# Joining two adjacency pieces on GpSimd before TensorE packs them, in a four-layer graph attention kernel

## The reference

```python
Wh = h @ W
e = (Wh @ a1)[:, None] + (Wh @ a2)[None, :]
e = jnp.where(e >= 0, e, ALPHA * e)
scores = jnp.where(adj > 0, e, NEG_BIG)
attention = jax.nn.softmax(scores, axis=1)
return attention @ Wh
```

## Time and profile before

| | |
|---|---|
| median of 3 executions | 4015.39 us (4013.88 to 4015.58) |
| the profiled execution, its own time | 4017.89 us |
| its span, first to last instruction | 4016.0 us |
| mean granted TensorE clock | 0.991 |
| layer 0 within the span | about 72 to 1107 us |
| instructions | 88535 |

### The profile page before, as it was taken

How to read it: one execution, slowest core, us unless ns; L and a number is a source line. 1 busy time by engine, 2 the same in 40 slices (tenths; PEclk the granted TensorE clock), 3 DMA queues, 4 the chain that set the end, 5 groups by cost and what they waited for, 6 DMA issues and landing times.

```text
span 4016.0 us, 88535 instructions
## 1 busy us (share of the span) xinstructions
PE 3924.8 (98%) x37901; PEld 3914.9 (97%) x37901; DVE 3621.3 (90%) x7914; ACT 1128.7 (28%) x2397; POOL 10.2 (0%) x98
## 2 busy tenths in 40 slices
PE   6999999999999999999999999999995999999999
PEld 6999999999999999999999999999995999999999
DVE  6888888888889999999998999999997999999998
ACT  6666666666641111111133111111112000000000
POOL 0000000000000000000000000000000000000000
PEclk9999999999999999999999999999997999999999
DMA  7787878787700000000001000000000000000000
GB/s 221 263 273 261 273 260 274 260 269 265 240 12 14 17 12 17 14 17 12 14 12 56 17 14 16 12 14 17 12 12 11 12 14 17 14 14 14 17 14 12
DMA packets 163146, 332.41 MB, mean 83 GB/s; under 512 B 12608, under 2 KB 87488, under 8 KB 162752
## 3 DMA queue, kind: packets, MB, share of 16 engines
q1 hardware_dynamic: 162752, 326.75, 24.8%
HBM read 305.53 MB, written 21.17 MB: 81 GB/s over the span
## 4 chain that ended last, share of the span: by engine, by line
PE 95%; DVE 2%; ACT 2%; issue 1%; POOL 0%; DVEq 0%; POOLq 0%; ACTq 0%
PE acc L1047 90%; PE ps_pack L983 2%; PE ps_wh L1065 1%; ACT vals L1219 1%; PE ps_wh L1059 1%; DVE q L676 0%; DVE q L842 0%; DVE q L850 0%; DVE vals L558 0%; DVE mask L649 0%; ACT adj_bf L1146 0%; DVE q L538 0%; PE acc L1109 0%; PE ps_bc L1022 0%; PE acc L1001 0%
## 5 line engine op out<-in xcount | busy, mean ns | idle before, releaser
L1047 PE MATMUL acc<-vals,q 128*128 128x129 f32 x32640 | 3731.2, 276 | 8.3 <-DVE q L676 8.3
L1047 PEld LDWEIGHTS acc<-vals,q 128*128 128x128 f32 x32640 | 3679.7, 192 | 9.9 <-issue 9.2
L676 DVE SCALAR_TENSOR_TENSOR q<-rrow,R,mask 128x512 f32<-128x512 f32 x3968 | 2840.6, 749 | 227.0 <-PE acc L1047 78.5
L1146 ACT ACTIVATE adj_bf<-adj_int,threshold 128x1024 bf16<-128x1024 int32 x512 | 584.2, 1143 | 119.5 <-PE ps_pack L983 79.0
L649 DVE TENSOR_SCALAR mask<-bits 128x512 uint16<-128x512 uint16 (+1 forms) x2080 | 444.5, 292 | 8.7 <-DMA rrow<-rows 4.6
L1230 ACT ACTIVATE xnew<-acc,rec 128x128 f32<-128x128 f32 x248 | 70.4, 365 | 899.3 <-DVE rec L707 802.9
L983 PEld LDWEIGHTS ps_pack<-packer,adj_bf 128*128 128x128 bf16 x4096 | 140.7, 96 | 8.1 <-ACT bits L1153 3.5
L983 PE MATMUL ps_pack<-packer,adj_bf 128*128 128x32 bf16 x4096 | 142.6, 176 | 4.3 <-ACT bits L1153 3.3
L1237 ACT ACTIVATE e<-xnew 128x512 f32<-128x512 f32 x48 | 30.3, 631 | 397.6 <-DVE xnew L737 314.2
L1250 ACT ACTIVATE e<-xnew,nm,rs 128x128 f32<-128x128 f32 x193 | 79.4, 481 | 216.9 <-DVE nm L530 216.9
L1245 ACT ACTIVATE sd<-ve 128x4 f32<-128x4 f32 (+1 forms) x49 | 9.9, 202 | 363.3 <-DVE ve L511 363.3
(11 more groups left out here) (186 smaller groups left out, 853.6 us busy)
## 6 DMA issues: line engine op xcount, KB each, us to landing
adj_int<-in_adj_dram SPq DMA_DIRECT2D x512, 512.0 KB, 4.7
rrow<-rows SPq DMA_DIRECT2D x60, 256.0 KB, 3.2
x_between_layers<-xnew SPq DMA_DIRECT2D x32, 256.0 KB, 4.0
xin<-x_between_layers SPq DMA_DIRECT2D x32, 256.0 KB, 2.7
xin<-in_x_dram SPq DMA_DIRECT2D x16, 256.0 KB, 4.8
wh_of_layer<-wh SPq DMA_DIRECT2D x1, 4096.0 KB, 16.9
x_of_layer<-xnew SPq DMA_DIRECT2D x16, 256.0 KB, 2.3
xin<-x_of_layer SPq DMA_DIRECT2D x16, 256.0 KB, 2.7
```

The lines of the kernel that those rows point to most:

```text
L676: nc.vector.scalar_tensor_tensor(q[:, j % RING, :], row, column(R_, t), mask[:, c % 2, j, :], ALU.max, ALU.mult).then_inc(q_ready, 1)
L1047: last = nc.tensor.matmul(to, q[:, j % RING, b * P:(b + 1) * P], vals[:, t, :], start=first, stop=(t == KT - 1 or g.two and t == EARLY - 1 ...
L1146: nc.scalar.activation(adj_bf[:, n % BIN_RING, :], adj_int[:, n % ADJ_RING, :], ACT.Sign, bias=threshold[:, 0:1], accum_out=degree_parts[: ...
```

## The change

GpSimd gets a function `joined(n)`. It waits until pieces n and n + 1 (two blocks of rows, same columns) are converted, multiplies the second by 4 in place, waits for that, and adds it to the first in place. As the powers of two of block b + 1 are four times those of block b, the packing matmul of the joined piece with the packer of block b yields the sum of both packings. TensorE waits for `adj_joined` in place of `adj_binary`, packs the first slot of each pair alone, and raises `adj_packed` by 2. GpSimd does the first 8 joins ahead of the first maximum over partitions, the joins of pieces 16 to 501 ahead of the second, and the last five pairs ahead of the third.

```diff
+            def joined(n):
+                pool.wait_ge(adj_binary, n + 2)
+                first, second = adj_bf[:, n % BIN_RING, :], adj_bf[:, (n + 1) % BIN_RING, :]
+                nc.gpsimd.tensor_scalar(second, second, 4.0, None, ALU.mult).then_inc(adj_times_4, 1)
+                pool.wait_ge(adj_times_4, n // 2 + 1)
+                nc.gpsimd.tensor_tensor(first, first, second, ALU.add).then_inc(adj_joined, 1)
+
             starts = [WHOLE[0], SOON[1], LATE[1], SOON[2], LATE[2]]
+            for n in range(0, LEAD * QP, 2):
+                joined(n)
             for n, to in enumerate([scales(st)[0][:, :] for st in starts] + [found[:, 0:1], found[:, 1:2], S[:, :]]):
+                if n == SOON[1].n:
+                    for i in range(LEAD * QP, GROUPS * PIECES - LEAD * QP + 6, 2):
+                        joined(i)
+                if n == LATE[1].n:
+                    for i in range(GROUPS * PIECES - LEAD * QP + 6, GROUPS * PIECES, 2):
+                        joined(i)
                 pool.wait_ge(smax_ready, n + 1)
                 nc.gpsimd.partition_all_reduce(to, smax[:, :], P, RMAX).then_inc(S_ready, 1)
...
             def pack(v, c, n):
                 if n == 0:
                     need(pe, bits_ready, v * CHUNKS + c)
-                for i in range(n, n + BATCH):
-                    pe.wait_ge(adj_binary, v * PIECES + (c * QP + i + 1))
+                for i in range(n, n + BATCH, 2):
+                    pe.wait_ge(adj_joined, (v * PIECES + c * QP + i) // 2 + 1)
                     for t in range(PT):
                         at = (i // BLOCKS * PT + t) * WORDS
                         last = nc.tensor.matmul(ps_pack[:, at:at + WORDS], adj_bf[:, i % BIN_RING, t * P:(t + 1) * P],
                                                 packer[:, i % BLOCKS, :], start=(i == 0 and t == 0),
-                                                stop=(i == QP - 1), skip_group_check=True)
-                    last.then_inc(adj_packed, 1)
+                                                stop=(i == QP - 2), skip_group_check=True)
+                    last.then_inc(adj_packed, 2)
```

More of the change, by code:

```diff
@@ L285, in build @@
         adj_binary = sem("adj_binary")
+        adj_times_4 = sem("adj_times_4")
+        adj_joined = sem("adj_joined")
         adj_packed = sem("adj_packed")
```

## The result

The changed kernel takes 4663.32 us (median of 3 executions, 4662.97 to 4663.39) against 4015.39 before: 1.1614 times as long, 95% interval 1.1592 to 1.1637. The forecast was 4615, range 4100 to 4880. In this document a run given with one time is a single execution; nine executions of the kernel before lie between 4013.50 and 4018.22 us.

What follows compares the result with a forecast made beforehand. TensorE bounds the kernel before; after the change VectorE and GpSimd were to share one resource. 4017.89 + 583 (sweeps) + 15 (start-up) + 2 (stall at layer 0's end), less 2.5 for the median, gives 4615 us, range 4100 to 4880.

Steps and rivals of the forecast that it cites:

- The bound and the slack: Layer 0 sweeps: TensorE bounds at 4.06 us a period, 0.40 of it packing; VectorE works 3.39, 0.67 to spare.
- Who pays for a join: Layer 0: VectorE's product with two SBUF inputs and a GpSimd read lock each other out; VectorE has 0.47 us spare.
- case (a): Kernel before: the all-reduce to S_early, issued behind a product of L676, was held about 0.53 us until that product ended.
- case (b): Kernel before: an unpacking issued behind 64 GpSimd memsets takes 1.44 us instead of 291 ns, ending 0.15 after them.
- The price of a join: GpSimd's multiply and add per pair: streams of 0.89 and 1.78 us plus 0.70 fixed, 3.4 us when alone.
- The sum: Layer 0 sweeps: VectorE's 3.39 plus 2.67 plus half of 0.70 makes 6.41 us a period against 4.06, +583 us.
- Start-up: Eight pairs ahead of layer 0: 6.6 us apart instead of 5.12, 10 us, plus some 3 before the all-reduce; +15 taken.
- A finer sharing: Layer 0: engines alternate element by element, 5.4 us a period, +332, some 4365 us; with a partial hold, chance 0.20.
- Nobody held: Layer 0: GpSimd reads leave products alone, TensorE stays the bound, 3978 us; held below break-even included, chance 0.13.
- The clock: Layer 0: TensorE's clock at 0.50 makes its work 7.7 us a period, +905, about 4940; with dear GpSimd, chance 0.07.
- GpSimd dearer than its memsets: Layer 0 joins: GpSimd far slower than its memset rows, streams of 4.45 us, 5055 us; with the clock, chance 0.07.

Runs made afterwards that it cites:

- the multiply aside: Kernel before, with GpSimd multiplying 1024 bf16 elements on scratch once per pair for 208 pairs, nothing waiting for it: 4025.82 us.
- the add aside: Kernel before, with GpSimd doing a two-input add on scratch once per pair for 208 pairs, nothing waiting for it: 4225.22 us.
- the row in PSUM: Changed kernel, with products of groups 1 to 14 of layer 0 reading their row from PSUM instead of SBUF: 4576.37 us.
- that run's counterpart without joins: Kernel before, with the same products of layer 0 reading their row from PSUM: 4015.31 us against 4018.06.
- the run with the multiply off the chain: Changed kernel with ScalarE writing odd pieces four times as large, plus a GpSimd multiply on scratch behind each of 208 adds: 4480.92 us.
- three pairs of four: Kernel before, with VectorE joining three of four pairs in the sweeps, ScalarE writing odd pieces four times as large: 3981.51 us, ratio 0.9913.
- the run with the add alone: Changed kernel with the multiply moved into ScalarE's conversion, so that GpSimd does only the add: 4289.85 us.
- the run with memsets aside: Kernel before, with GpSimd doing a memset of 1024 elements on scratch once per pair for 208 pairs: 4014.3 us.

## Why the prediction was right, and where it was not

**The bound and the slack.** Right. VectorE had 0.67 us a period to spare: the multiply aside, a hold of about that size, cost 11 us, the add aside cost 210. One step proves less than it says: 260/4 = 65.0 "agrees" only because the stretch was chosen 260 us long. A period is 4.14 with the transposes, of which VectorE works 3.45.

**Who pays for a join.** Right in its main point, which no row of before showed: a product behind a read by GpSimd is held. What was taken over from the other order (case (a)) is now shown three times: by the 2.6 us products beside an add, by the memset that holds no product, and by the row in PSUM, with which none is held. The Trainium skill's rule (SBUF — State Buffer, Who interferes with whom) is borne out in the two inputs and in reads against writes. Its whole-instruction lock is borne out by the add and not by the multiply, which holds for 0.8 us of its 2.8; there the measurement decides. One SBUF input alone doesn't keep an instruction free: the unpacking of L668 has only one and takes 665 ns in the mean beside the joins of the run with the row in PSUM, against 288 in that run's counterpart without joins. The same section names the modes with two ports for that, against any GpSimd instruction, which is also what covers case (b), a memset that reads nothing; no run here varies the mode.

**The price of a join.** Here the working was off, in both directions. The holds: I had 0.89 for the multiply and 1.78 for the add, plus 0.35, in sum 3.02. Measured are 0.78 and 1.87 in the instances above, 2.65, and in the mean 0.67 to 0.88 and 1.64 to 1.69 (the 0.88 by the same sum from the run with the multiply off the chain). So the streams worked out from the memset rows came close to the holds. But its own time was taken as 3.4 us a pair, and it is 2.77 + 2.11 = 4.9 alone and 5.4 beside VectorE. The add was well sized (2.11 against 1.78 + 0.35). The multiply is the one mis-sized term: 2.77 against 0.89 + 0.35. It holds VectorE for under a microsecond, but whoever waits for its result waits for all of it.

**The sum.** +583 for the sweeps against 601.3 measured in layer 0, of which 5.6 are the second wait of the all-reduce. The closeness is luck. The sum said 6.41 a period, VectorE's work and holds laid end to end. In the changed kernel these come to 5.80, VectorE is idle for the other 0.73, and the 6.53 is the chain's: GpSimd's two instructions and its wait for ScalarE. The prediction had dismissed that path: "GpSimd alone would be cover enough (3.4 in a period of 3.86)". The sentence that failed is that one: with 4.9 us GpSimd is no cover even if no product were ever held, as the row in PSUM shows at 4576. The lock that the prediction reasoned from is there and has a price, and an add beside VectorE pays it in full (210 us). In the changed kernel, as the run with the row in PSUM shows, it acts mostly through GpSimd, whose instructions it lengthens by 0.42 us a pair.

**Start-up.** I took +15; it is +44. The mechanism was right (the join goes in series, for the transposes stand behind the pack), but pairs are 10.0 us apart and not 6.6: seven times 5.0 = 35 instead of 10. Half of the 3.4 us missing from that chain is the join: 4.9, with its waits 5.1, instead of 3.4. The other half comes from a step that the prediction left out, the projections of L1021, for whose copy ScalarE waits ahead of the second conversion:

```profile
65.97 1.09 PE L1013 MATMUL acc<-ident,vals 128*128 128x128 f32 x4
...
66.86 1.94 PE L1021 MATMUL ps_wh<-w_sb,hT 128*128 128x130 f32 x8
...
69.38 1.15 ACT L1166 ACTIVATE adj_bf<-adj_int,threshold 128x1024 bf16<-128x1024 int32 x1
```

The first join adds 4.8. The rest, 4.3, is the wait of 5.78 us ahead of the all-reduce, of which the prediction said nothing.

**Rivals.** A finer sharing is out for the add, which keeps VectorE out until its end; the multiply's hold is a partial one. Nobody held is out. The clock: the granted clock of layer 0 fell to 0.91 from 1.00 as TensorE fell to 71% busy. It is not far below 1, and TensorE's products are 4.9% of the chain from 100 to 1750 us, so most of it hides under the waits; no run isolates it. GpSimd dearer than its memsets was true: a memset of 1024 elements takes 0.95 us, the multiply 2.77. But at 5055 that was added to VectorE's work and so priced too high.

**What stays open.** Why the multiply of 1024 elements takes 2.77 us when it holds VectorE for 0.8 was not tried. Nor was a deeper ring, or a copy of the words placed later in ScalarE's order. The share of the drain in the chain's 6.17 is read from GpSimd's waits for ScalarE and not shown by a run; the timeline puts it down to ScalarE's order rather than to the four slots of the ring.

## What to carry to other kernels

Before work goes to GpSimd beside a VectorE that streams two SBUF inputs, compare what the other engine would be *held* with what it would take to do the work itself: here 1.87 us against 0.68 for the same add. Then price GpSimd's instruction twice, once as a hold and once as latency on the path of whoever waits for it, since the two can differ threefold. A predicted time that comes out near may still name the wrong bound: look whether the engine that the sum fills is in fact busy throughout. And a saving that is worth 0.20 us a pair is best paid for from an engine's slack, as far as the slack reaches and no further (three pairs of four, not all), at a point of its program where it is sure to be ahead.

## What the runs showed of the hardware that was not expected

- GpSimd multiplies 128 x 1024 bf16 by a constant in 2.77 us where VectorE leaves it alone, and adds two such tiles in 2.11. The one-input instruction is the dearer one.
- The multiply holds a two-input product of VectorE for 0.78 us and then, though it runs on for some 2 us, no longer. The add holds one for up to 1.87. It works the other way too: beside two-input products the two instructions take 3.06 and 2.32 us, with the products' row in PSUM 2.82 and 2.15.
- A product with its row in PSUM is never held (896 of them, 754 ns at the most), and reading the row from there costs nothing (746 ns).
- An all-reduce over partitions that follows a multiply or an add of GpSimd started 5.6 to 6.0 us after a MODIFY_POOL_CONFIG (5.78 and 5.62 in the changed kernel, 6.03 in the run with the add alone). With the MODIFY_POOL_CONFIG at 16.6 us and idle time behind it, nobody waited. In the run with memsets aside no further one stands in the trace.
